# Second wide attention layer: Q tiles for up to three batches instead of two, and a V tile behind the second turn in slots without a Q tile

## The reference

```python
q = (decoder_query @ Wq).reshape(B, Sq, H, Dh)
k = (encoder_key_value @ Wk).reshape(B, Skv, H, Dh)
v = (encoder_key_value @ Wv).reshape(B, Skv, H, Dh)
q = rope(q)
k = rope(k)
...
scores = jnp.einsum('bqhd,bkhd->bhqk', q, k)   # after the transposes, q scaled
attn = jax.nn.softmax(scores, axis=-1)
out = jnp.einsum('bhqk,bkhd->bqhd', attn, v).reshape(B, Sq, H * Dh)
out = out @ Wo
x = decoder_query + out                        # then a layer norm
```

## Time and profile before

| what | value |
|---|---|
| time, median of 3 runs (lowest, highest) | 1988.24 us (1985.15, 1994.93) |
| the profiled execution: time, span | 1996.91 us, 1995.1 us |
| mean granted clock of TensorE, share of full speed | 0.983 |
| PE busy, share of the span | 1889.0 us, 95% |
| PEld, DVE, ACT, POOL busy | 82%, 67%, 66%, 29% |
| POOL busy in the slices of the second wide layer | 7 to 8 tenths |

### The profile page before, as it was taken

One profiled execution on the slowest core, in us unless ns is written; L12 is line 12 of the kernel. 1 busy time (PEld: TensorE's weight loads), 2 busy tenths in 40 slices (PEclk: granted clock), 3 DMA queues, 4 the chain that ended last, 5 costly groups with the idle time before them and its releaser, 6 DMA issues. The chain is left out here.

```text
span 1995.1 us, 50397 instructions
## 1 busy us (share of the span) xinstructions
PE 1889.0 (95%) x18558; PEld 1633.8 (82%) x18558; DVE 1339.7 (67%) x3063; ACT 1314.3 (66%) x3157; POOL 573.8 (29%) x732
## 2 busy tenths in 40 slices
PE   7799899898999999999999999999999997999998
PEld 6577777897888888888888888888888877777776
DVE  5577776546555555555567778778778764677775
ACT  4577677456665656556666767777777773777775
POOL 3232321000000000000047777777777731000000
PEclk8899999999999999999999999999999997999999
DMA  5543442203111111211212101101101102443441
GB/s 155 154 141 124 145 140 79 93 1 114 38 53 36 47 44 36 59 36 39 65 31 75 31 27 44 31 26 45 31 26 45 30 14 74 124 130 122 131 133 54
DMA packets 124829, 140.75 MB, mean 71 GB/s; under 512 B 46732, under 2 KB 114476, under 8 KB 124588
## 3 DMA queue, kind: packets, MB, share of 16 engines
q1 hardware_dynamic: 124300, 137.01, 23.0%
q10 hardware_dynamic: 288, 0.51, 0.1%
HBM read 88.20 MB, written 49.28 MB: 69 GB/s over the span
## 5 line engine op out<-in xcount | busy, mean ns | idle before, releaser
L646 ACT ACTIVATE L_P<-PS,MX 100x361 f32<-100x361 f32 x512 | 253.2, 566 | 134.5 <-DVE MX L776 134.5
L776 DVE TENSOR_REDUCE MX<-PS 100x2 f32<-100x722 f32 x256 | 219.9, 901 | 52.1 <-PE PS L526 52.0
L1988 POOL TENSOR_TENSOR wide_AC<-wide_T,wide_COSM 128x362 f32<-128x362 f32 x128 | 138.7, 1084 | 262.5 <-issue 137.0
L538 PE MATMUL PP<-CON,L_P 100*128 100x100 f32 x1536 | 180.9, 254 | 31.4 <-DVE L_PT L783 27.5
L538 PEld LDWEIGHTS PP<-CON,L_P 100*128 100x128 f32 x1536 | 148.7, 142 | 52.4 <-ACT L_P L646 39.5
L1632 ACT ACTIVATE wide_P<-wide_P,MX 100x361 f32<-100x361 f32 x256 | 149.8, 588 | 57.5 <-DVE MX L1774 56.0
L1632 ACT ACTIVATE wide_P<-PS,MX 100x361 f32<-100x361 f32 x256 | 140.5, 563 | 65.1 <-DVE MX L1779 65.1
L1493 PEld LDWEIGHTS PS<-CON,wide_P 100*128 100x128 f32 x1536 | 158.6, 141 | 23.0 <-ACT wide_P L1632 4.1
L1493 PE MATMUL PS<-CON,wide_P 100*128 100x100 f32 x1536 | 174.4, 250 | 1.5
L1506 PEld LDWEIGHTS PP<-wide_PT,wide_V 128*64 128x64 f32 (+1 forms) x3072 | 136.0, 136 | 32.6 <-issue 32.5
L1506 PE MATMUL PP<-wide_PT,wide_V 128*64 128x100 f32 (+1 forms) x3072 | 161.1, 253 | 0.2 <-ACT wide_PT L1640 0.2
(11 more groups left out here) (254 smaller groups left out, 5547.5 us busy)
## 6 DMA issues: line engine op xcount, KB each, us to landing
strips<-L_KS SPq DMA_DIRECT2D x256, 90.5 KB
L_KA<-strips SPq DMA_DIRECT2D x64, 362.0 KB, 3.1
wide_RB<-recip SPq DMA_DIRECT2D x128, 100.0 KB, 3.0
kept<-L_CTH SPq DMA_DIRECT2D x16, 361.0 KB, 5.0
kept<-L_CTL SPq DMA_DIRECT2D x16, 361.0 KB, 5.6
C<-ctx_t SPq DMA_DIRECT2D x16, 361.0 KB, 3.1
halves<-wide_CTH SPq DMA_DIRECT2D x16, 361.0 KB, 4.5
halves<-wide_CTL SPq DMA_DIRECT2D x16, 361.0 KB, 5.0
```

Of the source, the lines that this page charges most:

```text
L538: last = nc.tensor.transpose(PPB[:, n, SQ * t:SQ * t + SQ], P[:, (4 * g + 2 * i + n) % 8, 128 * t:128 * t + 128], ident[0:SQ, 0:SQ])
L646: nc.scalar.activation(P[:, (4 * g + j) % 8, 0:SK], PSB[0:SQ, j, 0:SK], ACT.Exp, bias=MX[:, s % 2, 4 * q + j:4 * q + j + 1], scale=1.0).th ...
L776: nc.vector.tensor_reduce(MX[:, s % 2, 4 * q + 2 * i:4 * q + 2 * i + 2], PSB[0:SQ, 2 * i:2 * i + 2, 0:SK], AX.X, ALU.max, negate=True).the ...
L1988: nc.gpsimd.tensor_tensor(ac, src, c, ALU.mult)
```

## The change

The second wide layer gets the first one's groups: 2, 2, 3, 3, 3 and 3 batches. Its 64 Q tiles of 200 columns become 16 of 200 and 32 of 300. Each tile has one place only (QH and QL are as large as before), so a tile p is made after the slot in which the batch before uses its place: Q 0 to 4 of a group in the slots of the batch before it (1, 2, 1 and 1 tiles), Q 5 and 6 in slot 0 and Q 7 in slot 1 of the group's first batch. In slots with no late job the last V tile of "mid" moves behind the second turn, a rule that stood in the code before and now finds such slots in the second layer too. For both layers the split of Q 3, 4 and 5 over the slots is shifted by one place (`Q_AHEAD`, `Q_WITHIN`).

```diff
-            QH, QL = local("QH", [128, 24 * SQ], f32r), local("QL", [128, 24 * SQ], f32r)
+            QH, QL = local("QH", [128, 8, 3 * SQ], f32r), local("QL", [128, 8, 3 * SQ], f32r)
...
-            GROUPS = {0: 2, 2: 2, 4: 3, 7: 3, 10: 3, 13: 3, **{s0: 2 for s0 in range(B, NS, 2)}}
+            GROUPS = {s0 + l: n for l in (0, B) for s0, n in ((0, 2), (2, 2), (4, 3), (7, 3), (10, 3), (13, 3))}
...
-            Q_AHEAD, Q_WITHIN = {0: (0,), 1: (1, 2), 2: (3, 4), 3: (5,)}, {0: (6,), 1: (7,)}
+            Q_AHEAD, Q_WITHIN = {0: (0,), 1: (1, 2), 2: (3,), 3: (4,)}, {0: (5, 6), 1: (7,)}
...
-                if s + 1 in GROUPS and s + 1 < B:
+                if s + 1 in GROUPS:
                     late += [("Q", s + 1, p) for p in Q_AHEAD[d]]
-                if s in GROUPS and 0 < s < B:
+                if s in GROUPS and s > 0:
                     late += [("Q", s, p) for p in Q_WITHIN.get(d, ())]
-                if s == B - 1:
-                    late += [("Q", B, 2 * d), ("Q", B, 2 * d + 1)]
-                if s >= B and s % 2 == 0 and s + 2 < NS:
-                    late.append(("Q", s + 2, 4 + d))
-                if s > B and s % 2 and s + 1 < NS:
-                    late.append(("Q", s + 1, d))
-                if d == 3 and s + 2 in GROUPS and s + 2 <= B:
+                if d == 3 and s + 2 in GROUPS:
                     late += [("X", s + 2, k) for k in range(KE)]
-                if d == 3 and s + 3 in GROUPS and s + 3 > B:
-                    late += [("X", s + 3, k) for k in range(KE)]
...
             def q_no(s, p):
-                return q_order.index(("Q", START_OF[s], p)) + 1
...
-                return W[:, width * slot:width * slot + q_columns(s0)]
+                return HP * STARTS.index(START_OF[s]) + p + 1
```

More of the change, by code:

```diff
@@ L1273, in wide_layers @@
                            14: ("V", 15, 5)}
-            q_order = [k for k in job_no if k[0] == "Q"]
             def q_no(s, p):
-                return q_order.index(("Q", START_OF[s], p)) + 1
[L1280 to L1284, removed]
-                return W[:, width * slot:width * slot + q_columns(s0)]
+                return HP * STARTS.index(START_OF[s]) + p + 1
             def x_no(s, k):
@@ L1485, in scores @@
                             for n, r in halves:
-                                last = nc.tensor.matmul(score_bank(g, n)[0:SQ, 0:SKE], q_at(Q_, s, p)[r, q], K_[r, p, :], start=m == 0, stop=m == 2)
+                                last = nc.tensor.matmul(score_bank(g, n)[0:SQ, 0:SKE], Q_[r, p, q], K_[r, p, :], start=m == 0, stop=m == 2)
                         last.then_inc(Z["scored"], 1)
@@ L1577, in rotated_high @@
                         act.wait_ge(Z["joined"], r + 1)
-                        hi, n, done = (KH[:, p, :], SKE, "k_high") if kind == "K" else (q_at(QH, s, p), q_columns(s), "q_high")
-                        nc.scalar.activation(hi, AC[:, r % NB, 0:n], ACT.Copy).then_inc(Z[done], 1)
+                        hi, n, done = (KH, SKE, "k_high") if kind == "K" else (QH, q_columns(s), "q_high")
+                        nc.scalar.activation(hi[:, p, 0:n], AC[:, r % NB, 0:n], ACT.Copy).then_inc(Z[done], 1)
                     def key_or_query(key, before):
@@ L1584, in key_or_query @@
                         if not rope(s):
-                            hi, n, done = (KH[:, p, :], SKE, "k_high") if kind == "K" else (q_at(QH, s, p), q_columns(s), "q_high")
-                            plain_high(key, hi, n, done)
+                            hi, n, done = (KH, SKE, "k_high") if kind == "K" else (QH, q_columns(s), "q_high")
+                            plain_high(key, hi[:, p, 0:n], n, done)
                             return
@@ L1750, in key_or_query @@
                             m = q_columns(s)
-                            plain_low(key, q_at(QL, s, p), q_at(QH, s, p), m, "q_high", q_no(s, p), "q_low")
+                            plain_low(key, QL[:, p, 0:m], QH[:, p, 0:m], m, "q_high", q_no(s, p), "q_low")
                     def query_turn(key):
@@ L1995, in rotated_low @@
                         m = q_columns(s)
-                        nc.gpsimd.tensor_tensor(q_at(QL, s, p), AC[:, r % NB, 0:m], q_at(QH, s, p).bitcast(fp32),
+                        nc.gpsimd.tensor_tensor(QL[:, p, 0:m], AC[:, r % NB, 0:m], QH[:, p, 0:m].bitcast(fp32),
                                                 ALU.subtract).then_inc(Z["q_low"], 1)
```

## The result

| | before | after |
|---|---|---|
| median of 4 runs each (lowest, highest) | 1990.34 us (1985.15, 1994.93) | 2010.56 us (1999.55, 2024.03) |
| the profiled execution: time, span | 1996.91, 1995.1 us | 1999.55, 1997.5 us |

The ratio of the changed kernel to the one before is 1.0094, with a 95% interval of 1.0067 to 1.0121: 18.7 us of 1988.24, or 13.3 to 24.1. The forecast was +9.4 us and 1998. The changed kernel is slower, by about twice what was forecast.

A forecast was written before the change was run, and what follows sets the result against it. PE, busy 95% of the span, was taken as the bound. Waits of 38.6 us instead of 23.4 (+15.2) and -5.8 of PE work gave +9.4 us, so a median of 1998 us, range 1980 to 2011.

The forecast's parts named there:

- likeliest case: Second layer's groups: Q 7 comes late and the clock falls; 1998 us, own range 1990 to 2009, chance 0.52.
- worse: Rival: waits at their upper bounds or clock falls twice as long, +9 to +18, 2007 to 2016 us; chance 0.13.
- PE -5.8: PE work in batches 15 to 30: fewer, wider Q tiles cost 39.0 us instead of 44.8, 5.8 less.
- Q 7 late, 18.4 us: Second scores of slot (s,3), six groups: PE waits for Q 7's low half on POOL, 18.4 us in all.
- Clock falls, five of six: Behind the new waits PE's clock halves for 3.3 us, costing 1.65 each; five of six, 8.3 us.
- Sign (c): Profile after: PE's clock at 0.5 for 3.4 us behind most of the waits for Q 7.
- The slot ahead of a group, 6.7 us: Slot (s,3) one batch ahead of five groups: scores wait for ACT's PT, 1.4 us in four, 1.1 in one.
- what the change heals: Most old waits go with their cause, with slot (15,3)'s 3.18 us; batch 15 keeps 2.7 of 7.3 us.
- Slots (s,1) and (s,2), 2.5 us: These slots of the six groups: waits of 0.4 us each kept, 2.5 us in all.
- Batch 15: Five Q tiles instead of eight, 2.7 of 7.3 us of waits left; near 40 us instead of 46.6.
- The clock holds: Rival: Q 7 late, but no clock falls behind its waits; +1.1 us, 1989 us, chance 0.20.
- Q 7 is there in time: Rival: POOL ends Q 7's low half in time; -17.3 us, 1971 us, chance 0.15; decides at about 1 us a group.

The follow-up runs named there:

- e3: Changed kernel with the second layer again in eight groups of two batches (tiles of 200 columns), new slots kept: ratio to the kernel before 1.0106, median 2012.8 us.
- e6: Changed kernel with DVE joining the Q tiles of the slot before only after shuffling the slot's own K tiles: ratio to the kernel before 1.0042, median 2002.28 us.
- e10: Changed kernel with ACT making the second PT ahead of V tile 5's copy in slot (s,2) of the second layer: ratio to the kernel before 1.0116.
- e8: Changed kernel with Q tiles' low halves between the two K tiles on POOL and Q joins behind the shuffles on DVE: ratio to the kernel before 0.9953.
- e4: Changed kernel with the last V tile kept ahead of the second turn in batches 16 to 29: ratio to the kernel before 1.0127, median 2018.91 us.
- e1: Changed kernel with Q 7 made in slot (s,0) and Q 5 in slot 3 of the batch ahead: ratio to the kernel before 1.0043, median 2000.7 us.
- e2: Changed kernel with Q tiles' low halves between the slot's two K tile multiplications on POOL: ratio to the kernel before 1.0007, median 1993.96 us.
- b3: Kernel before with Q joins behind the shuffles on DVE and low halves between the K tiles on POOL: ratio to the kernel before 0.9930, median 1981.53 us.
- e5: Changed kernel with PE's two weigh steps between the two pairs of scores in (s,3) of each group's first batch: ratio to the kernel before 1.0028.

## Where the forecast held and where it did not, step by step

**The mechanism of the likeliest case came true, its number did not.** Q 7 is late in all six groups and PE waits for it. The sum was +9.4 us, the trace shows +14.4 in the stretch, and all runs +18.7. The median of 2010.6 lies in the 2007 to 2016 of the rival "worse", but by another road: no wait for Q 7 reached the bound of 4.5 us and each fall lasted 3.4 us, while the slot ahead of a group, 3.2 us, went over its bound of 2.0. Direction and main cause are right. Four terms were mis-sized, two too high and two too low, and that the total stayed inside the range, by 0.4 us, is in part luck.

**"PE -5.8"** holds. Slot (20,1), with one tile of 300, and (21,1), with none, have no idle time between their ends:

```profile
1218.98:1229.64 10.66, 10.66 (x97) 1.00 0.01 2
1257.44:1267.28 9.84, 9.84 (x93) 1.00 0.01 3
```

That is 0.82 us for a tile of 300 columns without the X transposes; e3's slot (18,1) with one of 200 takes 10.49, so 0.65. With these, 64 x 0.65 - 16 x 0.65 - 32 x 0.82 = 5.0. (By the same 0.65 the waits of before come to 26.6 us, not to the 23.4 that were booked.) The Trainium skill ("TensorE: Matmul & The Clock Gate", "Back-to-back issue gap") gives a formula for an isolated matmul by which 0.2 to 0.3 us would be left of the term, an estimate (six matmuls of 200 columns come to 0.52 us by it, not to the 0.53 of the forecast). The rows of this case, 0.65 and 0.82 us a tile, decide against it.

**"Q 7 late, 18.4 us"**: 14.2 us of idle time, which by the forecast's own way of counting (0.17 more at each) is 15.2. From batch 18 on it is 2.6 to 2.8 us against the 2.9 and 3.3 forecast, in batch 16 1.8 against 2.3. The chain is as it was described, but the difference has another reason than a fast POOL. In (20,2) the multiplications start 6.96 us into the slot, later than the 6.1 of before, and take, with the low half, 4.36 us where 4.24 was measured before and some 4.5 forecast. What shortened the wait is that slot (20,2) itself took 8.2 us instead of the 7.0 forecast, since PE already waited there for Q 5: a part of the chain's lateness was spent one slot earlier.

**"Clock falls, five of six"** was wrong: two of six in this profile, none to seven in the stretches of the kernels above. As a mean over runs the term can't be read from one profile. By the clocks of all the runs the changed kernel loses some 4 us more than the kernel before; with the one fall that was booked as healed (1.7) that makes about 6 of the 8.3 us, a rough figure as said above. Sign (c), a fall behind most of the waits, is not there.

**"The slot ahead of a group, 6.7 us"** is the term that failed most. The wait for PT was forecast as 1.4 us and is 1.33 to 1.39 of idle time ahead of the four groups of three, and 0.71 instead of 1.1 in batch 17. But a second wait of 1.3 to 1.6 us (0.7 in batch 17), for the bank behind the join of Q 3, comes in the same slot and was not in the sum; it makes the term 3.2 us in four groups and 1.7 in that of batch 18, 14.5 in all. The step that failed is in the forecast's own words "what the change heals": the 3.18 us of slot (15,3) was taken as healed because fewer Q tiles are made there, while its rule (DVE joins a Q tile ahead of its own shuffles, and POOL is late with that tile when two low halves are ahead of it) was met again in each slot behind two Q tiles, and left 1.5 us in (15,3) itself. e6 shows it, and e10 shows that it is this one that ends last.

**"Slots (s,1) and (s,2), 2.5 us"**: the waits for Q 5 alone are 3.9 us of idle time in five slots, and e8, with the low halves moved, has (s,2) shorter by 0.8 to 1.0 us in each group of three.

**Batch 15** takes 40.4 us; 33.7 + 5 x 0.70 + 2.7 = 39.9 was forecast. **Batches without Q tiles** take 34.2 to 34.4, near the floor of 33.7, but only because the V tile stands behind the turn: e4 puts that at 1.4 to 1.6 us a batch. The forecast had it inside its floor without knowing, since batch 30 already had the rule before the change. **The first layer** costs nothing, as forecast: a group of three takes the same 108.0 us.

**The rivals.** "The clock holds" came true in four groups of six in one profile and still gave a slower kernel: without any fall in either, the stretches are 12.7 us apart, mostly since the +1.1 us lacked the second wait. "Q 7 is there in time", with its mark of about 1 us a group, was tried by e1 and e2: with no wait for QL at all e1 is still at 1.0043, and e2, at about 1 us a group, at 1.0007. So e2 bears the mark out, but the 17 us of gain that were to come with no wait at all did not come in e1, where the waits behind the join and for PT stood and grew.

**Open.** Why the same idle time is followed by a fall of the clock in one group and not in the next; and what of the quarter of a per cent between e8 and b3 is the two waits for QL and PT, since no kernel removes both.

## What to carry to other kernels

When a change moves a tile closer to its reader, follow it over every queue of its chain and ask on each what stands ahead of it that could stand behind: here the low halves two multiplications earlier on POOL and the joins two shuffles later on DVE were worth 1.4%, more than the loss they were to repair, and half of that was to be had without the change. When a stall of before is counted as healed, take its rule (which queue waits for what, under which load) and look for each place of the new order that meets it. And of two waits in one slot, look at the last one's cause first: here shortening the first gave its gain back some 8 us later.

## What the runs showed of the hardware

The clock's answer to idle time is not settled by its length. Windows of the changed kernel: PE idle, then the 3.4 us behind it, in slots (18,3) and (20,3).

```profile
1155.39:1157.86 2.47, 0.00 (x0) 0.03 (x1) 1.66 (x6) 2.06 (x6) 2.47 (x4) 1.00 0.69 202
1157.90:1161.30 3.40, 3.40 (x31) 2.71 (x31) 2.17 (x7) 1.60 (x6) 1.56 (x3) 0.50 0.20 71
...
1238.61:1241.06 2.45, 0.00 (x2) 0.03 (x1) 1.47 (x6) 2.08 (x6) 2.45 (x4) 1.00 0.68 201
1241.10:1244.50 3.40, 3.40 (x39) 3.02 (x40) 2.65 (x9) 1.92 (x7) 1.55 (x3) 1.00 0.19 68
```

The idle times of 2.47 and 2.45 us, with PE busy ahead of both, were followed by different levels: the first by 1.2 GHz (0.50), the second by 2.4 GHz. In e3 four of the seven waits of 2.45 to 2.47 us were followed by a fall and three were not. Shorter ones can be, too: in e8 a wait of 1.37 us in slot (23,3) was followed by 3.4 us at 0.50, from 0.7 us behind its end, and one of 1.49 us in (29,3) was not.

Kernels with such waits can spread more: 24 us in 4 runs of the changed kernel and 20 us in 10 of e6, which keeps the six waits for Q 7, against 9 us in 10 of e5, where each is cut in two. But it is no rule: the 4 runs of e3, with seven such waits, lie 2.5 us apart. The mean clock explains how far the changed kernel's runs lie apart; that it is the falls behind these waits which differ from run to run is likely but not shown, since only one run of each kernel has a profile.
